# Queries and keys made transposed and split ahead of each attention, expert weights loaded during attention

## The chip, the cores and the metric

One core of a Trainium2 chip runs the whole program, a two-layer transformer block in one launch. Its engines are TensorE (PE), VectorE (DVE), ScalarE (ACT), GpSimd (POOL) and SyncE (SP, which here only issues DMAs). The metric is the device time of the core in microseconds: lower is better. The time before is the median of three runs; beside it there is one profiled execution, from which all rows come.

## The reference

The input x has 4 batches of 1024 tokens, 256 wide, so 4096 tokens. Each attention has 16 heads of 16.

```
x = x + LN(attention0(LN(x)))            # softmax(q k^T / 16) v, then w_out; no mask
x = x + LN(moe0(LN(x)))                  # twice: z += sum over 2 groups of expert(rmsnorm(z)); 8 experts, 512 wide, silu
x = x + LN(attention1(LN(x)))            # q,k,v with biases; scores + slope*(key - query), causal; w_out, bias
x = x + LN(balanced_experts(LN(x)))      # every expert gets 512 tokens; 1024 wide, gelu
```

Everything is float32. The scores are made to float32 accuracy from `fp32r` operands: a number is split in a high part (its `fp32r` rounding) and a low part (the rest), and q k is high x high + high x low + low x high, which one product of 64 rows per head can hold: the rows of q are [extra, high, high, low], those of k [extra, low, high, high] or the like, 16 rows each, and 5 extra rows (`AUG`) carry the running max and, in the second attention, the position term.

## The kernel before

The program is a chain of stages with a barrier of all engines between them: `ln_qkv` (tag qkv0), `attention` (att0), `attn_post`, then twice `rms_logits`, `route`, `experts`, then `combine_qkv` (qkv1), `attention` (att1), `attn_post`, and the assigned experts. The order on each engine is that in which the code is written; semaphores join the engines. `Mem` holds a stage's buffers and semaphores.

**qkv stages.** 32 tiles of 128 tokens. For each: norm (VectorE), two transposes (`turn`), products with 768 columns of w (`product`: the tile's xT is stationary, w moves), copy of the PSUM tile (`y_out`), a store of 384 KB to `qkv`. In qkv1 a product with two rows of ones adds the bias (L1239), in a part of 512 and one of 256 columns.

**Attention.** It works on couples of two heads, 8 for each batch and 32 in all. One couple takes a slot on TensorE, of NS steps: 16 in the first attention, 12 in the second, causal one. In a slot three couples are worked on: couple e has its products `qk` (L233) and `pv` (L249), the next couple m and the one behind it have their `scores` (L221) for the row maximum. `qk(n)` fills a PSUM bank that ScalarE's exp (L317) reads, `scores` fills one that VectorE's maximum (L357, causal: L363) reads; both draw on a ring of three banks S, and TensorE waits in L228 and L215 for the reader of the bank that it takes next. At step NS-4 `turn_max` (L263) transposes the couple's max, VectorE copies it to mT (L386), and SP's `place` (L115) puts it as a row into qT, for which the first `qk` of the next slot waits (m_placed). `finish` (L257) transposes the output for the division by the sum of exps (L371 to L377).

qT and kT are made inside the attention: SP loads rows of q and k (`load_qk`, L108) for two couples at once, GpSimd's `natural` splits them into qn and kn (token by token), TensorE's `fill` transposes half of one (four transposes, L206) into the bank TP, and ScalarE's `evac` (L314) copies it out. There are four fills in a slot: at n=0, at QUERIES0 = 2*CHUNK0 (8 and 4), at KEYS0-1 (10 and 6), and at NS-2. TP is shared with `finish`; `t_bank_read` (L199) waits for its last reader:

```
def fill(s,f,half):
    if f==1 and half==0: pe.wait_ge(nat_ready[s],1)...
    t_bank_read()
    for t in range(4): mm=pe.transpose(TP[...],(kn,qn)[f][:,s,4*half+t]...,identr[:])
    mm.then_inc(half_full,1)
```

**rms, route, experts.** `rms_logits` normalises 32 tiles and makes the routing logits. In the first of the two, ScalarE issues the loads of w1 and w2 (8 of 1 MB) ahead of its work, and every second tile carries one of 16 parts of 1024 columns: a high copy (ScalarE, L830) and the subtraction of it (VectorE, L859). Each of these stages loads its own constants, and VectorE and TensorE wait for them first. `route` makes one-hots for 64 columns of tokens in chunks of 8 (VectorE L1022, ScalarE L925), sums them on TensorE (L934), and writes `source`, `target` and the expert of each tile. `experts` gathers 128 rows for each of 72 tiles (GpSimd, L1063).

## Time and profile before

| what | us |
|---|---|
| median of three runs | 3442.67 (3439.02 to 3446.1) |
| profiled execution, its own time | 3440.81 |
| its span in the trace | 3438.9 |
| qkv0 from | 0 |
| att0 from | 109.24 |
| first post stage, first rms, route, experts from | 1002.65, 1116.9, 1200.1, 1267.65 |
| second rms, route, experts from | 1559.9, 1634.15, 1701.57 |
| qkv1 from | 1993.04 |
| att1 from | 2157.87 |
| second post stage from | 2850.5 |
| TensorE, VectorE, ScalarE, GpSimd busy | 2745.7, 1968.0, 1642.4, 931.7 |

A stage runs from the first event behind one barrier to that behind the next, and all engines wait for the slowest at each. TensorE is busy for 80% of the span, but that is a mean over stages with different limits; a stage must be read for itself. Times in rows are us from the span's start.

### The profile page before, as it was taken

What the parts mean: (1) busy time and instruction counts of PE and PEld (TensorE: products, weight loads), DVE (VectorE), ACT (ScalarE), POOL (GpSimd) and SP (SyncE); (2) the same over time, 40 slices, a digit from 0 to 9 for tenths busy, and PEclk for the clock granted to TensorE, in tenths of its full rate; (3) what the DMA queues carried; (4) which work ended last, traced back from release to release, by engine and by line L of the source; (5) the groups of instructions that cost most, each with busy time, mean ns of one, the idle gap of its engine ahead of it and who ended that gap; (6) DMA issues with size and microseconds to landing.
All of it is one profiled execution on the core that took longest, in us unless ns stands there. A gap on an engine that the chain in (4) does not pass through costs nothing. (4 is left out here: it accounts for less than half of the span.)

```text
span 3438.9 us, 63399 instructions
## 1 busy us (share of the span) xinstructions
PE 2745.7 (80%) x16332; PEld 1631.3 (47%) x16333; DVE 1968.0 (57%) x4576; ACT 1642.4 (48%) x2593; POOL 931.7 (27%) x1637
## 2 busy tenths in 40 slices
PE   8699999999975449995399959688888887718887
PEld 5333333333333438884388824344444444515554
DVE  4478887888845353335433354477666764555641
ACT  3277777777754434433344335366666663301212
POOL 1211111111016105541055444222222213302333
PEclk9699999999996559995599979799999996659999
DMA  6201010010023402225022257211111104322331
GB/s 167 58 20 25 12 25 19 19 25 19 12 58 100 156 10 70 68 61 150 16 67 69 64 148 195 52 26 25 25 31 28 28 10 118 114 96 69 98 99 60
DMA packets 367444, 216.00 MB, mean 63 GB/s; under 512 B 285262, under 2 KB 347218, under 8 KB 366295
## 3 DMA queue, kind: packets, MB, share of 16 engines
q1 hardware_dynamic: 231832, 99.25, 11.2%
q10 hardware_dynamic: 117568, 62.92, 6.1%
q0 software_dynamic: 17920, 52.46, 4.8%
q8 instruction: 43, 0.70, 0.1%
q14 instruction: 81, 0.66, 0.1%
HBM read 130.13 MB, written 85.98 MB: 63 GB/s over the span
## 5 line engine op out<-in xcount | busy, mean ns | idle before, releaser
L317 ACT ACTIVATE att_pr<-att_S 128x1024 f32<-128x1024 f32 (+1 forms) x896 | 835.9, 941 | 428.2 <-ACTq L324 426.4
L357 DVE TENSOR_REDUCE att_mparts<-att_S 128x2 f32<-128x1024 f32 x640 | 776.8, 1224 | 170.3 <-DVEq L353 166.3
L233 PE MATMUL att_S<-att_qT,att_kT 64*128 64x512 f32 (+3 forms) x1792 | 430.6, 473 | 45.4 <-PEq L228 41.8
L249 PE MATMUL att_OP<-att_pr,att_vn 128*32 128x512 f32 (+3 forms) x3584 | 451.9, 565 | 1.0 <-PEq L243 0.7
L221 PE MATMUL att_S<-att_kT,att_qT 64*128 64x512 f32 (+3 forms) x1792 | 390.9, 431 | 73.6 <-PEq L215 61.9
L233 PEld LDWEIGHTS att_S<-att_qT,att_kT 64*128 64x128 f32 x1792 | 175.0, 184 | 471.3 <-issue 460.3
L169 POOL COPY att_vn<-att_raw 128x256 f32<-128x256 f32 x64 | 25.4, 396 | 1150.0 <-POOLq L168 1150.0
L221 PEld LDWEIGHTS att_S<-att_kT,att_qT 64*128 64x128 f32 x1792 | 188.0, 191 | 172.7 <-issue 166.3
L363 DVE CUSTOM_DVE_ANT_0 att_unused<-att_S,att_mask 128x128 f32<-128x128 f32 (+3 forms) x512 | 228.4, 488 | 71.9 <-DVEq L353 71.8
L1063 POOL DMA_INDIRECT experts_xs<-scaled,ffn_source x144 | 140.3, 974 | 368.5 <-SPq L1056 172.2
L1163 DVE COPY experts_y<-experts_Y 128x256 f32<-128x256 f32 x144 | 61.1, 424 | 225.1 <-DVEq L1162 225.1
L1137 ACT ACTIVATE experts_hh<-experts_TH 128x512 fp32r<-128x512 f32 x144 | 86.1, 598 | 205.2 <-ACTq L1136 205.2
L1069 POOL DMA_INDIRECT mixed<-experts_y,ffn_target x144 | 146.2, 1015 | 88.6 <-issue 46.7
L1160 DVE TENSOR_TENSOR experts_hl<-experts_TH,experts_hh 128x512 fp32r<-128x512 f32 x144 | 99.6, 692 | 117.8 <-DVEq L1158 117.1
L1140 ACT ACTIVATE experts_h<-experts_H 128x512 f32<-128x512 f32 x144 | 86.1, 598 | 125.3 <-ACTq L1139 125.3
L1405 PE MATMUL ffn_Y<-ffn_w,ffn_hT 128*128 128x256 f32 x512 | 127.3, 399 | 8.8 <-PEq L1404 8.8
L1400 PE MATMUL ffn_H<-ffn_xT,ffn_w 128*128 128x512 f32 x256 | 120.4, 626 | 14.7 <-PEq L1398 8.7
L653 PE MATMUL post_Y<-post_w,post_aT 128*128 128x256 f32 x256 | 104.0, 549 | 33.4 <-PEq L651 33.4
L457 POOL TENSOR_TENSOR post_s<-post_s,post_half 128x2 f32<-128x2 f32 x128 | 96.2, 752 | 118.4 <-POOLq L629 112.5
L249 PEld LDWEIGHTS att_OP<-att_pr,att_vn 128*32 128x32 f32 x3584 | 72.2, 108 | 109.6 <-issue 105.2
L314 ACT ACTIVATE att_qT<-att_TP 128x512 fp32r<-128x512 f32 x128 | 76.1, 594 | 90.7 <-ACTq L312 90.7
L371 DVE TENSOR_REDUCE att_osum<-att_TP 128x136 f32<-128x272 f32 x128 | 56.2, 439 | 99.9 <-DVEq L369 99.9
(290 smaller groups left out, 4977.3 us busy)
## 6 DMA issues: line engine op xcount, KB each, us to landing
qkv<-qkv_y ACTq DMA_DIRECT2D x64, 384.0 KB, 3.9
att_raw<-qkv SPq DMA_DIRECT2D x96, 256.0 KB, 3.2
ffn_w<-in_w ACTq DMA_DIRECT2D x20, 1024.0 KB, 13.4
rows<-post_rows ACTq DMA_DIRECT2D x32, 384.0 KB, 2.8
ao<-att_aon SPq DMA_DIRECT2D x32, 256.0 KB, 2.3
post_at<-ao SPq DMA_DIRECT2D x64, 128.0 KB, 3.0
scaled<-rms_zs SPq DMA_DIRECT2D x64, 128.0 KB, 1.7
rms_rows<-mixed SPq DMA_DIRECT2D x32, 256.0 KB, 3.1
```

The lines of the kernel that those rows point to most:

```text
L221: mm=pe.matmul(S[:,b,h,at:at+n],qT[r,s,qt*128:qt*128+128],kT[r,s,half*512:half*512+n],start=True,stop=True)
L233: mm=pe.matmul(S[:,b,h,f:512],kT[r,s,kt*128:kt*128+128],qT[r,s,c*512+f:c*512+512],start=True,stop=not diag)
L249: mm=pe.matmul(OP[32*j:32*j+32,f:512],vn[:,s,kt,h,:],pr[:,n%4,h,f:512],start=kt<2,stop=g in last_groups,skip_group_check=True)
L317: nc.scalar.activation(pr[:,n%4,:,f:512],S[:,ring["e",n],:,f:512],ACT.Exp,scale=exp_scale).then_inc(s_free[ring["e",n]],1)
L357: nc.vector.tensor_reduce(mparts[:,s,:,2*qt+half],S[:,b,:,0:width(qt,half)],AX.X,ALU.max).then_inc(end,1)
L363: nc.vector.tensor_tensor_reduce(unused[:,2*i+h,0:n],S[:,b,h,at:at+n],mask[:,512-n:512],1.0,-3.0e38,ALU.add,ALU.max,mparts[:,s,h,2*qt+half ...
L653: mm=pe.matmul(Y[:,u%4,0:DIM],aT[:,u%2,128*k:128*k+128],w[:,k,:],start=k==0,stop=k==KC-1 and not last)
L1063: nc.gpsimd.indirect_dma_start(out=xs[:,t%R,:],out_offset=None,in_=zs_d,in_offset=bass.IndirectOffsetOnAxis(ap=source[:,t:t+1],axis=0)).th ...
L1069: nc.gpsimd.indirect_dma_start(out=y2_d,out_offset=bass.IndirectOffsetOnAxis(ap=target[:,t:t+1],axis=0),in_=y[:,t%RY,:],in_offset=None, bo ...
L1160: V.tensor_tensor(hl[:,u%2],TH[:,u%2,:],hh[:,u%2].bitcast(F32),ALU.subtract).then_inc(hT_ready,1)
L1400: mm=pe.matmul(H[:,c%2,:],w1[:,e%2,k,128*c:128*c+128],xT[:,k,:],start=k==0,stop=k==KC-1)
L1405: if c<FC: pe.matmul(Y[:,t%2,0:DIM],hT[:,c,128*t:128*t+128],w2[:,e%2,c,:],start=c==0,stop=False)
```

## The change

- `ln_qkv` and `combine_qkv` make q and k transposed: `features` takes 128 columns of w as the stationary operand and xT of four tiles (512 tokens) as the moving one, four steps behind `turn`. ScalarE copies the product to its high part, VectorE subtracts for the low part, and both go to DRAM `qk` (two 2 KB pieces of a row, 512 KB in each of 32 stores). v is made and stored by itself (`values`). In qkv1 the bias of q and k is added in these two instructions, and only v's 256 columns keep the product with ones.
- `attention` has no `natural`, `fill`, `evac`. It has four operand sets of qT and kT. SP's `load_set` fills one from `qk` by rows: 12 loads of 16 rows of 4 KB, and 2 rows of zeros (att0) or 4 loads of position rows (att1). It is issued three couples ahead, when TensorE gives a set free at n=2, and stands ahead of `place` in SP's program. `scores` of a couple wait for `set_loaded`. At the start GpSimd clears qT, VectorE clears kT and writes its two rows of -1, and only then are sets free.
- In att0 SP issues, behind the first three sets and the first values and ahead of the first `place`, the loads of w1, w2 and seven constants that the ffn stages now hold. GpSimd splits w1 in eight parts, four behind the first values and four at the end.
- `rms_logits` of the first loop splits only w2, eight parts, at every third step; no stage of the ffn loads constants. In `route` two of eight one-hots are made on VectorE directly, and the tile counts come last. In `experts` four gathers are issued at once, and the first product comes ahead of the second transpose.

```diff
 attention
-        qn=sb("qn",[128,2,TILES,2,WIDE],F32R); kn=sb("kn",[128,2,TILES,2,WIDE],F32R); identr=sb("identr",[128,128],F32R)
-        qT=sb("qT",[128,2,SEQ],F32R)
+        SETS=4
+        qT=sb("qT",[128,SETS,SEQ],F32R); kT=sb("kT",[128,SETS,SEQ],F32R)
...
+                def load_set(b,pair):
+                    s=pair%SETS; done=set_loaded[s]
+                    sp.wait_ge(set_free,1).then_inc(set_free,-1)
+                    for m,T,high,both in ((0,qT,AUG,AUG+HD),(1,kT,AUG+2*HD,AUG)):
+                        for h in range(2):
+                            to=lambda row,n: T[64*h+row:64*h+row+n,s,:].bitcast(F32)
+                            parts=qk_d[m][:,bass.ds(b*HEADS+2*pair+h,1)].bitcast(F32)
+                            sp.dma_start(to(high,HD),parts[0,0]).then_inc(done,16)
+                            for x in range(2): sp.dma_start(to(both+HD*x,HD),parts[x,0]).then_inc(done,16)
+                            if causal: sp.dma_start(to(0,AUG),augr[AUG*(2*pair+h):AUG*(2*pair+h)+AUG,m,:].bitcast(F32)).then_inc(done,16)
+                            elif m==0: sp.dma_start(to(0,1),zeros[:].bitcast(F32)).then_inc(done,16)
...
+                    if not (last and c+3>=COUPLES): load_set(*later(c+3))
...
+                    if not (last and c+1>=COUPLES): place(c+1)
+                for c in range(3): load_set(0,c)
+                load_v(0,0)
+                if ahead:
+                    for k in range(KC): sp.dma_start(w1[:,k,:].bitcast(F32),w1_d[128*k:128*k+128,:]).then_inc(w_loaded[k],16)
+                    sp.dma_start(w2[:].bitcast(F32),w2_d.rearrange("(k p) n -> p k n",p=128)).then_inc(held_loaded,16)
+                    for tile,value in zip(held,held_d): sp.dma_start(tile[:],value).then_inc(held_loaded,16)
+                place(0)
...
+                    if x==0: pe.wait_ge(set_loaded[s],16*LOADS).then_inc(set_loaded[s],-16*LOADS)
...
-                        if m is not None and n==0: fill(m,0,1)
-                        if a is not None and n==QUERIES0: fill(a,1,0)
-                        if a is not None and n==KEYS0-1: fill(a,0,0)
-                        if a is not None and n==NS-2: fill(a,1,1)
+                        if prev is not None and n==2: pe.sem_inc(set_free,1)
...
+                nc.vector.memset(kT[:].bitcast(F32),0.0).then_inc(dve_done,1)
...
+                for h in range(2): nc.vector.memset(kT[64*h:64*h+1].bitcast(F32),-1.0).then_inc(keys_cleared,1)
...
 ln_qkv
+                def low(b,u):
+                    dve.wait_ge(high_ready,1).then_inc(high_ready,-1)
+                    done(nc.vector.tensor_tensor(hl[:,u%HB,1],Q[:,u%2],hl[:,u%HB,0].bitcast(F32),ALU.subtract))
...
+                def features(b,u):
+                    f=u%4
+                    pe.wait_ge(q_free,1).then_inc(q_free,-1)
+                    for k in range(KC):
+                        mm=pe.matmul(Q[:,u%2],w[:,k,128*f:128*f+128],xT[:,k,u//4,:],start=k==0,stop=k==KC-1)
+                pipelined(pe,[turn,values,None,None,features])
...
 rms_logits
-            for i in range(16):
-                q=i//4; at=slice(1024*(2*q+i%2),1024*(2*q+i%2)+1024); raw,high=flat[0:2] if i%4<2 else flat[2:4]
-                parts[SCALED+4+2*i]=(q if i%4==0 else None,raw[:,at],high[:,at])
+            for i in range(8): parts[SCALED+2+3*i]=slice(1024*i,1024*i+1024)
```

The first place is TensorE's program in the second attention, at steps 4 to 6 of a slot: `att_S<-att_qT,att_kT` is `qk`, `att_S<-att_kT,att_qT` is `scores`, `att_TP<-att_identr` a fill, `att_TP<-att_ident` is `finish`. Before:

```order
L233 MATMUL att_S<-att_qT,att_kT 128x512 x2
L221 MATMUL att_S<-att_kT,att_qT 128x128 x2
L221 MATMUL att_S<-att_kT,att_qT 128x256 x2
L206 MATMUL att_TP<-att_identr,att_qn 128x128 x4
L257 MATMUL att_TP<-att_ident,att_ot 128x128 x4
L233 MATMUL att_S<-att_qT,att_kT 128x512 x2
L221 MATMUL att_S<-att_kT,att_qT 128x384 x2
```

And now:

```order
L221 MATMUL att_S<-att_qT,att_kT 128x512 x2
L209 MATMUL att_S<-att_kT,att_qT 128x128 x2
L209 MATMUL att_S<-att_kT,att_qT 128x256 x2
L245 MATMUL att_TP<-att_ident,att_ot 128x128 x4
L221 MATMUL att_S<-att_qT,att_kT 128x512 x2
L209 MATMUL att_S<-att_kT,att_qT 128x384 x2
```

The fill is gone, and `finish` follows the `scores` directly; the rest stands as it stood.

The second place is SP's program in the first attention, from the identity (before) or from the end of the third set (now) to the first `place`, which is `att_qT<-att_mT`. Before:

```order
L101 DMA att_ident<-in_ident 128x128
L108 DMA att_raw<-qkv 128x8x64 x2
L111 DMA att_raw<-qkv 128x8x64
L108 DMA att_raw<-qkv 128x8x64 x2
L115 DMA att_qT<-att_mT 1x8x128 x2
```

And now:

```order
L118 DMA att_kT<-qk 16x1024 x2
L123 DMA att_raw<-v 128x8x64
L146 DMA ffn_w<-in_w_0 128x4096 x2
L147 DMA ffn_w<-in_w_0 128x4x2048
L148 DMA ffn_ident<-in_ident 128x128
L148 DMA ffn_wg<-in_w_route 128x2x12
L148 DMA ffn_nw<-in_norm_w 128x256
L148 DMA ffn_trif<-in_prefix 128x256
L148 DMA ffn_key<-in_order 128x128
L148 DMA ffn_jv<-in_starts 128x576
L148 DMA ffn_marks<-in_marks 128x192
L127 DMA att_qT<-att_mT 1x8x128 x2
```

Three loads of weights and seven of constants now stand ahead of the first `place`, on the same queue.

The third place is ScalarE's program in the first rms stage. Before:

```order
L821 ACTIVATE rms_sq,rms_ss<-l_z 128x256
L826 ACTIVATE rms_zT<-rms_T 128x256
L830 ACTIVATE ffn_w1h<-ffn_w 128x1024
L821 ACTIVATE rms_sq,rms_ss<-l_z 128x256
L826 ACTIVATE rms_zT<-rms_T 128x256
L821 ACTIVATE rms_sq,rms_ss<-l_z 128x256
L826 ACTIVATE rms_zT<-rms_T 128x256
L830 ACTIVATE ffn_w1h<-ffn_w 128x1024
```

And now:

```order
L779 ACTIVATE ffn_w2h<-ffn_w 128x1024
L772 ACTIVATE rms_sq,rms_ss<-l_z 128x256
L777 ACTIVATE rms_zT<-rms_T 128x256
L772 ACTIVATE rms_sq,rms_ss<-l_z 128x256
L777 ACTIVATE rms_zT<-rms_T 128x256
L772 ACTIVATE rms_sq,rms_ss<-l_z 128x256
L777 ACTIVATE rms_zT<-rms_T 128x256
L779 ACTIVATE ffn_w2h<-ffn_w 128x1024
```

A part stood at every second tile, sixteen in all; it stands at every third now, eight in all, and the eight weight loads ahead of the first square are gone.

## Rows read from the trace of the kernel before

**Rows 1.** Windows: engine busy time (x instructions), PEclk, DMA share, GB/s.
```profile
150.00:160.00 10.00, 8.78 (x36) 4.06 (x34) 8.38 (x7) 5.07 (x6) 2.64 (x7) 0.50 0.12 27
150.00:1000.00 850.00, 766.42 (x4835) 304.50 (x4833) 661.47 (x749) 604.22 (x698) 116.10 (x262) 0.99 0.08 18
2200.00:2850.00 650.00, 567.00 (x4817) 305.16 (x4813) 439.23 (x1353) 400.31 (x568) 127.23 (x320) 0.99 0.11 24
```
**Rows 2.** Line L263 in each attention: ns min/median/max, first and last start.
```profile
L263 PE MATMUL att_S<-att_ident,att_m x32: 269/269/370, 148.0 to 970.3; 128*16 128x128 f32 x32
L263 PE MATMUL att_S<-att_ident,att_m x32: 269/270/372, 2191.8 to 2821.5; 128*16 128x128 f32 x32
```
**Rows 3.** Timeline of TensorE, first attention: start, us, engine, line, operation [idle].
```profile
565.67 0.53 PE L206 MATMUL att_TP<-att_identr,att_qn 128*128 128x128 f32 x4
...
566.81 0.51 PE L221 MATMUL att_S<-att_kT,att_qT 64*128 64x512 f32 x2 [0.18 <-PEq L215]
```
**Rows 4.** Timeline of ScalarE, the same stretch.
```profile
565.64 1.02 ACT L317 ACTIVATE att_pr<-att_S 128x1024 f32<-128x1024 f32 x1 [1.28 <-ACTq L324]
```
**Rows 5.** Timeline of TensorE, second attention, n=4 and 5.
```profile
2430.31 0.63 PE L257 MATMUL att_TP<-att_ident,att_ot 128*128 128x128 f32 x4 [1.10 <-PEq L199]
...
2431.20 0.34 PE L221 MATMUL att_S<-att_kT,att_qT 64*128 64x384 f32 x2
```
**Rows 6.** Timeline of ScalarE, the same stretch.
```profile
2429.57 0.59 ACT L314 ACTIVATE att_qT<-att_TP 128x512 fp32r<-128x512 f32 x1
```
**Rows 7.** Timeline of SP, second attention.
```profile
2417.08 1.37 SPq L115 DMA_DIRECT2D att_qT<-att_mT  x2
2419.05 1.01 SPq L108 DMA_DIRECT2D att_raw<-qkv  x2
```
**Rows 8.** Timeline of VectorE, start of the first route stage.
```profile
1204.42 0.27 DVE L945 MEMSET route_zero<- 128x256 f32 x1 [5.33 <-DMA route_marks<-in_marks]
```
**Rows 9.** DMA queues of 1115:1145: packets, MB, share.
```profile
q10 hardware_dynamic: 1152, 8.39, 68.7%
```
**Rows 10.** Timeline of all engines, first placing of a max.
```profile
149.34 1.49 SPq L115 DMA_DIRECT2D att_qT<-att_mT  x2
...
152.51 0.80 PE L233 MATMUL att_S<-att_qT,att_kT 64*128 64x512 f32 x2 [0.82 <-PEq L228]
```
**Rows 11.** Timeline of ScalarE, first rms stage.
```profile
1121.43 0.42 ACT L821 ACTIVATE rms_sq<-l_z 128x256 f32<-128x256 f32 x1 [3.25 <-issue]
...
1135.31 0.38 ACT L826 ACTIVATE rms_zT<-rms_T 128x256 f32<-128x256 f32 x1 [0.62 <-ACTq L825]
...
1136.48 0.38 ACT L826 ACTIVATE rms_zT<-rms_T 128x256 f32<-128x256 f32 x1 [0.39 <-ACTq L825]
...
1140.66 0.38 ACT L826 ACTIVATE rms_zT<-rms_T 128x256 f32<-128x256 f32 x1 [1.39 <-ACTq L825]
...
1144.85 0.38 ACT L826 ACTIVATE rms_zT<-rms_T 128x256 f32<-128x256 f32 x1 [1.39 <-ACTq L825]
```
**Rows 12.** Timeline of ScalarE and VectorE, end of the first route.
```profile
1258.63 5.52 ACT L925 ACTIVATE route_named<-route_in_slot,route_zeros,route_marks 128x72 fp32r<-128x72 f32 x16 [0.15 <-ACTq L922]
...
1262.21 1.20 DVE L943 TENSOR_REDUCE route_ef<-route_ge 128x72 f32<-128x576 f32 x1
```
**Rows 13.** Timeline of GpSimd, start of the first expert stage.
```profile
1272.68 0.95 POOL L1063 DMA_INDIRECT experts_xs<-scaled,ffn_source  x1 [2.75 <-POOLq L1062]
```
**Rows 14.** Timeline of SP, start of the second rms stage.
```profile
1564.84 6.45 SPq L799 DMA_DIRECT2D rms_rows<-mixed  x6
```
**Rows 15.** Timeline of TensorE, first qkv stage.
```profile
61.70 2.75 PE L562 MATMUL qkv_Y<-qkv_w,qkv_xT 128*128 128x512 f32 x8
```
**Rows 16.** Timeline of TensorE, second qkv stage.
```profile
2060.92 0.50 PE L1239 MATMUL qkv_Y<-qkv_biasr,qkv_ones 2*128 2x512 f32 x1
...
2062.72 0.44 PE L1230 MATMUL qkv_T<-qkv_ident,qkv_xn 128*128 128x128 f32 x2
...
2066.60 0.44 PE L1230 MATMUL qkv_T<-qkv_ident,qkv_xn 128*128 128x128 f32 x2
```

More of the change, by code:

```diff
@@ L190, in _ @@
+                if ahead:
+                    for i in range(PARTS//2): split(i)
+                with pool.Fori(1,BATCH*GROUPS):
+                    group()
+                if ahead:
+                    for i in range(PARTS//2,PARTS): split(i)
+                    pool.wait_ge(low_done,PARTS)
+                    pool.wait_ge(held_loaded,16*(1+len(held)))
             @block.tensor
             def _(pe):
-                pe.sem_inc(nat_free[0],1); pe.sem_inc(nat_free[1],1); pe.sem_inc(v_free[0],1); pe.sem_inc(v_free[1],1)
+                pe.sem_inc(v_free[0],1); pe.sem_inc(v_free[1],1)
@@ L1217, in root_x @@
                     root(nc,pool,half,sx[:,n%R],pool_done,rootx)
-                for n in range(NT+3):
-                    for lag,stage in ((0,root_z),(3,root_x)):
+                for n in range(NT+2):
+                    for lag,stage in ((0,root_z),(2,root_x)):
                         if 0<=n-lag<NT: stage(n-lag)
@@ L1278, in _ @@
-                done(V.tensor_scalar(low[:],low[:],ident[0:2,1:2],None,ALU.mult))
-                done(V.scalar_tensor_tensor(out=biasr[:],in0=high[:].bitcast(F32),scalar=ident[0:2,0:1],in1=low[:],op0=ALU.mult,op1=ALU.add))
+                done(V_.memset(ones[:].bitcast(F32),1.0))
+                done(V_.tensor_copy(split[:],bias[:]))
+                done(V_.tensor_tensor(rest[:],bias[:],split[:].bitcast(F32),ALU.subtract))
+                done(V_.tensor_scalar(rest[:],rest[:],ident[0:2,1:2],None,ALU.mult))
```

601 lines of the change are left out of this document (267 added, 334 removed).

## Prediction

> **What bounds the kernel now.** I read the busy time by windows first, then the order of events inside one slot of each attention, then the starts of the stages. In the long middle of both attentions TensorE is busy nine tenths of the time, more than any other engine [rows 1]: 766 of 850 us in the first, 567 of 650 us in the second. So work off TensorE's path is worth nothing there, and work on it is worth its length, less what comes back as another wait. The transposes of the max (one in each slot) give the slot: (970.3 - 148.0)/31 = 26.5 us in the first attention, (2821.5 - 2191.8)/31 = 20.3 us in the second [rows 2]. Attention holds 1586 of the 3439 us. The other stages are short, and their starts are waits.
>
> **Steady slots, first attention.** Out go four groups of four transposes (L206), some 0.46 us of TensorE each, and four ScalarE copies. 4 x 0.46 x 31 would be 57 us if it all lay on the path. The order of events says otherwise. Each fill stands behind `scores` of an even step; ahead of the next `scores` TensorE waits for the bank that exp reads. Exp starts at 565.64 and takes 1.02; the `scores` that need its bank start at 566.81, 0.15 behind its end, and TensorE still waited 0.18 with the fill in the gap [rows 3, 4]. Without the fill the same `scores` start at the same time: the fill is covered by the exp. What is gained is where the ScalarE copy delays an exp. I take 0.2 us a slot, -6 in all, with 0 and 0.5 (-16) as its ends.
>
> **Steady slots, second attention.** Half of the exps are shorter than 1024 columns, and the cover is thinner. Behind a fill, `finish` (L257) at 2430.31 had waited 1.10 us for ScalarE to have copied the shared bank TP: the copy starts at 2429.57, behind an exp that ends at about 2429.67, and takes 0.59 [rows 5, 6]. `scores` of the next step start at 2431.20. Without fill and copy, `finish` starts 0.46 us earlier plus those 1.10, and `scores` then wait only for that exp's end plus 0.15, so till 2429.8: 1.4 us gained. The fill at n=6 has no `scores` of an odd step behind it and is bare, 0.46; that at n=10 is bare for 0.1, that at n=0 is hidden by VectorE's row max. That is 2.0 us a slot of TensorE's path. Part comes back: VectorE's masked row maxima are queued close behind, and TensorE meets them sooner. Bounds: 0.65 if only the 0.2 to 0.5 us rests survive, 1.8 if nearly nothing is given back. I take 1.1, for 31 slots -34 (-20 to -55).
>
> **Can the row loads keep up?** A slot now needs 14 loads (16 in the second attention, plus store and values in every second slot, 17 on average) on SP's queue ahead of `place`, where 3 stood in two slots. Two loads issue in 1.01 us, two of `place` in 1.37 [rows 7], so 0.5 us each, at worst 0.69. SP may begin at n=2, some 4 us into the slot, and the placed max needs about 1.4 + 1.7 us behind it: 4 + 17c + 3.1 us. At c=0.5 that is 15.6, at 0.69 18.8 us, both under 19.2. The 64 KB loads of 16 pieces of 4 KB are smaller than the 256 KB of 256-byte pieces that those rows show, so I take 0.5 and no cost. The Trainium skill (DMA: Bandwidth & Descriptors, Rules for kernel authors) says that under 64 KB one pays mostly overhead; at its fixed 2 us for each, one after another, the 16 loads would take 32 us and bound the slot, an estimate from that page. That is a rival below, priced from rows.
>
> **Starts of the attentions.** VectorE's memset of 256 columns takes 0.27 us [rows 8], some 0.83 ns a column above the fixed part; kT has 4096 columns, and three such memsets (all, then one row for each head) are 10.3 us. Only then may SP load. 14 issues of 0.5 and 2 us of landing: first `scores` at +19.4 us, against +17.5 before: +2. In the second attention the copy of the position rows (2048 columns, 1.7 us by the same rate) stands ahead too, and 16 issues: +4.
>
> **Weights ahead of the first `place`.** This is the term that speaks against the change. SP issues three sets (42 x 0.5 = 21 us), the values, then 8.39 MB of w1 and w2 and 0.80 MB of constants, and only then `place(0)`, on one queue. Before, eight weight loads moved 8.39 MB with 68.7% of the DMA time of 30 us, so 0.41 MB/us [rows 9]. The weights begin at +10.4+21.5+1.5 = +33.4 and end 22.6 us later, at +56. Before, `place` was issued at 149.34 (+40.1) and the first `qk` ran at 152.51 (+43.3) [rows 10]; now it could run at +45.2. If `place` is served behind the weights, `qk` starts at +56.5: 11 us more. If it is served beside them, 0. The trace of before has no small transfer behind megabytes on its own queue to read it from. By the Trainium skill (DMA: Bandwidth & Descriptors, Queues, rings and completion order) each DMA engine consumes the descriptors of one ring in order, which gives the 11; its rule that different rows are served in turn would have given 0 had the weights stood on another queue. I take 11. TensorE's granted clock was still 0.50 in 150:160 with the first couple under way [rows 1]; 11 us of idleness there keep it low longer. I add 3 us for it. Sum of the start: 2 + 11 + 3 = +16.
>
> **First rms stage.** ScalarE issued eight loads until 1121.43 before its first square; block start 1116.9, less 1.3 for the table load that stays: -3.1. A tile without a split takes 1.17 (1135.31 to 1136.48), two tiles with one split 4.19 (1140.66 to 1144.85) [rows 11]: a split costs 4.19 - 2.34 = 1.85. Eight of sixteen remain: -14.8. Together -18. The w1 splits run on GpSimd in the attention, idle there for most of the time: nothing.
>
> **Route, experts, second rms.** Route's VectorE waits for constants until 1204.42, 4.2 us behind its start at 1200.1 [rows 8]; these are held now: -4.2. ScalarE makes 16 one-hots in 5.52 [rows 12], 0.345 each; two of eight move to VectorE, whose pace then bounds: I take 0.3 of the possible 0.69 for 8 chunks, -2.4, and -1.2 for the first chunk's order. The tile counts, hidden until now, come behind the targets: a reduce of 1.20 [rows 12], a compare of the same tile and two short ones, I take +2.9. Per route -4.9, two: -9.8. Experts: the second gather waited 2.75 us [rows 13]; issued back to back, and the first product ahead of the second transpose: -2.5, twice -5. Second rms: rows are fetched at 1564.84 behind the constants though the stage begins at 1559.9 [rows 14]: -4.4.
>
> **The two qkv stages.** TensorE's columns stay the same: 2.80 us a tile in the first [rows 15]. But `features` lag four steps, so four steps run at VectorE's pace (I estimate 2.0) and four blocks of 1.75 are left at the end: 8.1 + 28 x 2.8 + 7 = 93.5 against 89.6: +4. In the second a tile takes 3.88 (2062.72 to 2066.60), with 0.43 for the bias product of 512 columns [rows 16], which goes; VectorE's own work grows by the 128x512 subtraction, 0.7, to about 3.55, just above TensorE's 3.45. 4 x 2.9 + 28 x 3.55 + 7 = 118 against 124.5, with 1.5 for the shorter bias preparation: -8. Ends: -14 and +2, the latter if the longer chain of waits (features, high, low, free) costs 0.3 a tile.
>
> **Sum.** 4 + 16 - 6 - 18 - 9.8 - 5 - 4.4 - 8 + 4 - 34 = -61. Against the profiled execution's 3440.8 that is 3380; the median of the runs lies 2 us above it, within their spread, so 3380 stands for it too.
>
> **Rivals.**
> (a) The fills were worth more: both attentions gain near their upper bounds (-16, -55) and `place` is served beside the weights (0, no clock loss). 3380 - 10 - 21 - 14 = 3335. For: VectorE was busy only 68% of the second attention. Against: waits for VectorE already stand between the steps. 0.17.
> (b) VectorE takes the fills' place in the second attention (about 0 there) or the qkv stages lose: 3380 + 34 = 3414, or 3390. The ffn stages alone still gain 37. 0.20.
> (c) Slower: issue of the row loads bounds the second attention. At c=1.0 us the slot is 4 + 17 + 3.1 = 24.1, +3.8 for 31 slots: 3380 + 34 + 118 = 3530. It decides from c = 0.83, where the slot is 21.2 us and all other gains are eaten. For: nothing that size was issued before. Against: no row above 0.69 in the steady part. 0.09. Another 0.02 for an issue cost near that point, where gain and loss cancel.
> (d) As summed, between 3350 and 3400: 0.52.
>
> **How the numbers follow.** 3380 is (d). The range takes in (a) and most of (b): 3332 to 3412. Some 0.2% (7 us) is what a measurement of this kernel can tell from no change. (a), (b) and (d) all lie below 3436: faster 0.89; the 0.02 is the same; (c) is slower, 0.09.
>
> **What would show it.** First `qk` of the first attention at +56 (right) or +45 (the queue serves `place` beside the weights). SP's issues near 0.5 us each. Slot of the second attention 19.2 us, of the first 26.3; behind `finish` no wait for ScalarE, more waits for VectorE. First rms 18 us shorter. Wrong if SP is still issuing when the max is ready, if waits for `set_loaded` show at TensorE, or if a qkv tile takes over 4 us.

## The result and the profile after

| | before | after |
|---|---|---|
| median of the runs on one chip | 3440.85 (3430.84 to 3446.1) | 3731.13 (3725.98 to 3736.39) |
| ratio | 1 | 1.0848 (1.0823 to 1.0874) |
| profiled execution, its span | 3440.81, 3438.9 | 3728.71, 3726.6 |

The kernel became 8.5% slower; the forecast was 3380, so 1.8% faster, with 3332 to 3412 as its range. Each kernel of the experiments was timed beside the kernel before on one chip. Its number is given against the median of the kernel before in that sitting (3431.7 to 3437), with the ratio and its 95% interval.

First the page of the changed kernel, its totals and TensorE's row of the 40 slices (one digit is 93 us), and behind them the same row of the kernel before (86 us):

```profile
PE 2744.7 (74%) x15276; PEld 1572.5 (42%) x15277; DVE 2021.0 (54%) x4669; ACT 1509.1 (40%) x2361; POOL 708.6 (19%) x1074
...
PE   5554888888887646996499946648888887736887
...
PE   8699999999975449995399959688888887718887
```

The rows hint where to look: the first three slices of the changed kernel hold TensorE at 5 tenths, where the first slice of the kernel before has 8, and those of its second qkv stage (slices 24 to 27) have 4 to 6. Other slices are as low in both kernels, so the stage lengths decide. They are taken, from one table load of ScalarE to the next (us; the terms of the forecast's sum beside them):

| stage | before | after | difference | forecast |
|---|---|---|---|---|
| qkv0 | 108.5 | 282.7 | +174.2 | +4 |
| att0 | 893.4 | 912.8 | +19.4 | +10 (start +16, steady -6) |
| rms0 | 83.2 | 64.1 | -19.1 | -18 |
| route0, route1 | 67.6, 67.4 | 65.8, 66.2 | -3.0 | -9.8 |
| experts0, experts1 | 292.2, 291.5 | 288.2, 287.3 | -8.2 | -5 |
| rms1 | 74.3 | 71.2 | -3.1 | -4.4 |
| qkv1 | 164.8 | 295.6 | +130.8 | -8 |
| att1 | 692.7 | 690.1 | -2.6 | -30 (start +4, steady -34) |
| post0, post1, ffn1 | | | -0.7 | 0 |

The differences add up to 287.7, and by so much the span is longer. The two qkv stages alone lose 305; the rest of the kernel gained 17. Each stage is read from one trace, and identical code does not take the same time in every trace: in the eight traces here whose second attention is that of the changed kernel, this stage takes 688.5 to 698.1. So its -2.6 is no difference from before.

**The first qkv stage.** The waits of the changed kernel from 0 to 330 us (engine, line, whose event ended the wait: us in total, times, longest):

```profile
DVE qkv_hl L490 <- DVEq L489: 184.4, 32, 7.3
PE qkv_T L504 <- PEq L502: 118.9, 30, 9.3
```

L490 is `low`, VectorE's subtraction; L489 is its wait for ScalarE's `high`. L504 is `turn`, which waits for the normalised tile. Each waits in each tile. One tile in the timeline (start, us, engine, line, operation, idle before):

```profile
104.67 0.60 ACT L533 ACTIVATE qkv_hl<-qkv_Q 128x512 fp32r<-128x512 f32 x1 [2.99 <-ACTq L532]
...
105.41 0.69 DVE L490 TENSOR_TENSOR qkv_hl<-qkv_Q,qkv_hl 128x512 fp32r<-128x512 f32 x1 [7.11 <-DVEq L489]
106.55 0.43 DVE L485 BATCH_NORM_STATS2 qkv_st<-qkv_xt 128x6 f32<-128x256 f32 x1 [0.44 <-DVEq L483]
...
107.71 0.41 DVE L494 TENSOR_SCALAR qkv_xn<-qkv_xt,qkv_st 128x256 f32<-128x256 f32 x1
...
108.42 0.66 PE L504 MATMUL qkv_T<-qkv_ident,qkv_xn 128*128 128x128 f32 x2 [3.96 <-PEq L502]
...
108.97 2.05 PE L511 MATMUL qkv_V<-qkv_w,qkv_xT 128*128 128x256 f32 x4
...
110.80 1.92 PE L517 MATMUL qkv_Q<-qkv_xT,qkv_w 128*128 128x512 f32 x2
...
114.63 0.60 ACT L533 ACTIVATE qkv_hl<-qkv_Q 128x512 fp32r<-128x512 f32 x1 [3.03 <-ACTq L532]
...
115.37 0.69 DVE L490 TENSOR_TENSOR qkv_hl<-qkv_Q,qkv_hl 128x512 fp32r<-128x512 f32 x1 [7.25 <-DVEq L489]
```

Read it as a ring: `low`, the statistics, `normal`, `turn`, `values`, `features`, `high`, `low`. From one `low` to the next 9.96 us pass, and little overlaps. From the sixth tile on, 8.0 to 10.4 us lie between one `turn` and the next, 9.2 on average. Before, a tile took 2.80. The granted clock is lower too. One window of the changed kernel's first stage (us, busy time of PE, PEld, DVE, ACT, POOL, then PEclk, DMA share, GB/s):

```profile
100.00:150.00 50.00, 29.73 (x55) 14.41 (x54) 9.34 (x25) 7.20 (x16) 2.74 (x5) 0.70 0.24 79
```

**The second qkv stage.** The waits of 2170 to 2440:

```profile
POOL qkv_sz L432 <- POOLq L1164: 152.8, 26, 8.6
DVE qkv_hl L1258 <- DVEq L1257: 150.1, 30, 7.8
ACT qkv_lnz L1206 <- ACTq L1205: 149.6, 31, 6.1
```

Three engines each wait some 150 us of 270. The profile names only the waiting line; what it waits for is read from the program: GpSimd's roots for VectorE's statistics, ScalarE's `ln_z` for the roots, VectorE's `low` (L1258) for ScalarE's `high`. `turn` starts at 2378.73 and again 9.10 us later, where it had come every 3.88 [rows 16]:

```profile
2378.73 0.66 PE L1181 MATMUL qkv_T<-qkv_ident,qkv_xn 128*128 128x128 f32 x2 [3.73 <-PEq L1178]
...
2387.83 0.66 PE L1181 MATMUL qkv_T<-qkv_ident,qkv_xn 128*128 128x128 f32 x2 [2.84 <-PEq L1178]
```

**The start of the first attention.** The stage begins at 283.43. SP's timeline from the weights to the first `place` (L127), which answers to [rows 10]:

```profile
321.87 1.90 SPq L148 DMA_DIRECT2D ffn_nw<-in_norm_w  x1
323.81 4.79 SPq L148 DMA_DIRECT2D ffn_trif<-in_prefix  x1
328.64 2.72 SPq L148 DMA_DIRECT2D ffn_key<-in_order  x1
331.40 0.43 SPq L148 DMA_DIRECT2D ffn_jv<-in_starts  x1
331.88 6.91 SPq L148 DMA_DIRECT2D ffn_marks<-in_marks  x1
338.90 1.49 SPq L127 DMA_DIRECT2D att_qT<-att_mT  x2
```

TensorE, the same stretch:

```profile
327.37 0.37 PE L250 MATMUL att_S<-att_ident,att_m 128*16 128x128 f32 x1 [2.04 <-PEq L249]
...
346.13 0.79 PE L221 MATMUL att_S<-att_qT,att_kT 64*128 64x512 f32 x2 [16.07 <-PEq L216]
```

The max was transposed at 327.37. SP was still issuing constants, and four of these issues held it 1.9 to 6.9 us where another of the same line takes 0.4. Before, the same load of `in_marks`, with no weights ahead of it, held SP for 0.43. `place` was issued at +55.5, and the first `qk` ran at +62.7, 19.4 later than before. The first `scores` had come at +22.9 (before +17.5). Ahead of them VectorE's timeline has the three memsets, which had been taken for 10.3 us in all and take 3.47 each with gaps:

```profile
284.37 3.47 DVE L310 MEMSET att_kT<- 128x4096 f32 x1 [5.12 <-PEq L29]
...
288.94 3.47 DVE L313 MEMSET att_kT<- 1x4096 f32 x1 [1.02 <-DVEq L312]
293.31 3.47 DVE L313 MEMSET att_kT<- 1x4096 f32 x1 [0.91 <-issue]
```

**The steady second attention.** Two windows, and two single microseconds of the second:

```profile
2700.00:2740.00 40.00, 33.29 (x284) 16.75 (x278) 29.26 (x90) 21.75 (x29) 0.88 (x3) 1.00 0.23 59
2900.00:2940.00 40.00, 34.23 (x270) 16.86 (x268) 27.72 (x84) 20.82 (x28) 0.80 (x2) 0.91 0.22 54
...
2902.00:2903.00 1.00, 0.01 (x1) 0.00 (x0) 0.84 (x4) 0.94 (x2) 0.00 (x0) 1.00 0.46 127
2903.00:2904.00 1.00, 0.86 (x6) 0.46 (x10) 0.81 (x2) 0.00 (x0) 0.00 (x0) 0.61 0.11 33
2904.00:2905.00 1.00, 1.00 (x8) 0.02 (x3) 0.71 (x4) 0.98 (x1) 0.00 (x0) 0.50 0.46 131
```

TensorE there, at step 7 of a slot:

```profile
2903.14 0.75 PE L221 MATMUL att_S<-att_qT,att_kT 64*128 64x512 f32 x2 [1.13 <-PEq L216]
2903.82 1.94 PE L237 MATMUL att_OP<-att_pr,att_vn 128*32 128x512 f32 x8
```

The same step ten slots earlier, and what VectorE and ScalarE did ahead of 2903.14:

```profile
2705.41 0.49 PE L221 MATMUL att_S<-att_qT,att_kT 64*128 64x512 f32 x2 [1.13 <-PEq L216]
2705.83 1.06 PE L237 MATMUL att_OP<-att_pr,att_vn 128*32 128x512 f32 x8
...
2901.93 1.02 ACT L291 ACTIVATE att_pr<-att_S 128x1024 f32<-128x1024 f32 x1
...
2902.28 0.55 DVE L332 CUSTOM_DVE_ANT_0 att_unused<-att_S,att_mask 128x384 f32<-128x384 f32 x1
```

The wait of 1.13 us stands in both. Three banks of S are handed out in turn, so this `qk` takes the bank of the `scores` of 384 columns at step 5. Its reader is VectorE's masked maximum, which ends at 2902.83. The exp that runs beside it reads another bank, that of step 6. So the wait is for VectorE. At 2705 the granted clock stays at 2.4 GHz and the eight `pv` take 1.06; at 2903 it falls to 1.2 GHz for some 3.6 us and they take 1.94. Slots of the first kind last 19.18 and 19.92 in turn, of the second 20.41 and 20.55; before, all took about 20.3 at a granted clock of 0.97 to 1.00. The wait stands in 30 slots. The clock held behind 13 of them and fell behind 17, the last 13 of the stage among these.

### The profile page after: what moved, and what is told of

The parts are those of the page before. It is cut to its first block and busy times, and to the rows that moved or that the text cites. A ratio compares the mean times of both kernels' runs of the same rounds, so it can differ in the third digit from the quotient of the medians.

```text
span 3726.6 us, 61821 instructions
## 1 busy us (share of the span) xinstructions
PE 2744.7 (74%) x15276; PEld 1572.5 (42%) x15277; DVE 2021.0 (54%) x4669; ACT 1509.1 (40%) x2361; POOL 708.6 (19%) x1074
## 5 line engine op out<-in xcount | busy, mean ns | idle before, releaser
L291 ACT ACTIVATE att_pr<-att_S 128x1024 f32<-128x1024 f32 (+1 forms) x896 | 826.2, 940 | 642.7 <-ACTq L297 640.8
L221 PE MATMUL att_S<-att_qT,att_kT 64*128 64x512 f32 (+3 forms) x1792 | 438.5, 479 | 138.2 <-PEq L216 132.3
L237 PE MATMUL att_OP<-att_pr,att_vn 128*32 128x512 f32 (+3 forms) x3584 | 466.8, 583 | 1.1 <-PEq L231 0.7
L490 DVE TENSOR_TENSOR qkv_hl<-qkv_Q,qkv_hl 128x512 fp32r<-128x512 f32 x32 | 22.1, 692 | 184.4 <-DVEq L489 184.4
L1380 PEld LDWEIGHTS ffn_Y<-ffn_w,ffn_hT 128*128 128x128 f32 x512 | 95.2, 194 | 32.2 <-issue 20.4
```

Source lines behind the costliest of these rows:

```text
L221: mm=pe.matmul(S[:,b,h,f:512],kT[r,s,kt*128:kt*128+128],qT[r,s,c*512+f:c*512+512],start=True,stop=not diag)
L237: mm=pe.matmul(OP[32*j:32*j+32,f:512],vn[:,s%2,kt,h,:],pr[:,n%4,h,f:512],start=kt<2,stop=g in last_groups,skip_group_check=True)
L291: nc.scalar.activation(pr[:,n%4,:,f:512],S[:,ring["e",n],:,f:512],ACT.Exp,scale=exp_scale).then_inc(s_free[ring["e",n]],1)
L1380: if c<FC: pe.matmul(Y[:,t%2,0:DIM],hT[:,c,128*t:128*t+128],w2[:,e%2,c,:],start=c==0,stop=False)
```

## The experiments

**The ring in the first qkv stage.** My theory was that `low` of tile n-5, which VectorE does in the same step as `normal` of n-1, waits for a product that TensorE does only behind `turn` of the tile that `normal` has just given. The rivals were that the work itself, the row stores of 2 KB pieces, or the lower granted clock bound the tile. One step more of lag keeps all work and all traffic:

```diff
-                pipelined(dve,[x_stats,normal,None,None,None,low])
+                pipelined(dve,[x_stats,normal,None,None,None,None,low])
```

> Only the first qkv stage is edited: VectorE takes `low` of a tile six steps behind, not five. Theory (a loop in program order): in one step VectorE runs the norm of tile n and then waits for the high copy of tile n-4, whose product stands behind the transposes of tile n on TensorE, so nothing overlaps and a tile costs the whole chain, 9 to 10 us. With one step more the loop is open: a tile then costs 2.9 to 3.3 us, the stage goes from 283 us to 105 to 120, the kernel from 3731 to 3555 to 3575. Rival A (the 512 KB stores and their landing set the pace) expects no change, since the stores are the same. Rival B (TensorE's lower granted clock, 0.7 to 0.83 here, lengthens the stage by itself) expects no change either, or some 20 us. Rival C (SP's order, where each load waits behind the store eight tiles older) expects a tile still above 6 us.

> The same edit with seven steps. If only the loop mattered, six and seven steps give the same within 5 us. If the wait for the high copy still shows at six, seven is up to 10 us shorter: VectorE then paces a tile at about 2.9 us. If SP's loads, which stand behind the store of the tile eight steps older, come too late for it, seven is slower than six and VectorE waits for x at its statistics.

Measured with six: 3585.96 against 3436.99, 1.043 (1.041 to 1.0451); with seven 3579.25, 1.0411 (1.039 to 1.0432). The stage falls from 282.7 to 131.9 and 127.5. One `None` is worth 151 us with every instruction and every store kept, so the ring is shown, and the granted clock is back at 1.00 (10 to 110 us; 0.77 in the changed kernel), so it had followed the ring. The size was a miss: 105 to 120 us had been expected of six, and 3555 to 3575 of the kernel. What remains is some 3.6 us a tile, TensorE with the kernel of six:

```profile
61.58 0.41 PE L504 MATMUL qkv_T<-qkv_ident,qkv_xn 128*128 128x128 f32 x2 [0.44 <-PEq L502]
...
65.10 0.41 PE L504 MATMUL qkv_T<-qkv_ident,qkv_xn 128*128 128x128 f32 x2 [0.25 <-PEq L502]
```

**The same cure in the second.** There ScalarE's step begins with `ln_z`, which waits for statistics that VectorE makes at the end of a step, and ends with `high`, for which VectorE waits at the start of the next.

```diff
                 def step(at):
+                    if at(7): high(*at(7))
                     if at(0): ln_z(*at(0))
...
-                    if at(7): high(*at(7))
```

> Only the second qkv stage is edited: in ScalarE's step the high copy comes first, ahead of ln_z, ln_x, the copy of the transposes and v. Theory: `low`, which stands first in VectorE's step, waits for a high copy that stands behind ln_z of the step before, which waits through GpSimd's root for the statistics at the end of that very VectorE step; the loop VectorE, GpSimd, ScalarE, VectorE makes 9.1 us a tile. With the high copy first a tile costs 3.6 to 4.5 us, the stage 295.6 goes to 130 to 160, the kernel to 3565 to 3600. Rivals A (stores) and B (clock) expect under 30 us of change.

Measured: 3709.99, 1.0791 (1.0764 to 1.0818). The stage fell by 19 to 276.2, where 130 to 160 had been expected. The waits of 2170 to 2420 show why:

```profile
ACT qkv_hl L1218 <- ACTq L1217: 162.0, 28, 7.0
...
DVE qkv_hl L1258 <- DVEq L1257: 123.7, 28, 7.1
```

ScalarE's wait went from `ln_z` to `high` itself: it now stands first, ahead of `turned`, and waits for `features`, which has only two Q banks and stands behind the `turn` of that step. The edit moved the ring and did not open it. My expectation had looked at one engine's order and not at the whole ring.

> Both edits (six steps in the first stage, high copy first in the second). Theory: the two gains add up, 3731 - 170 - 145 = 3415, with 3395 to 3440; the rest of the change is then seen to be worth 0 to 45 us against the kernel before. A rival in which one stage's slowness only hides a wait of the other is excluded by the barriers between stages, so a sum that is missed by over 10 us would need another cause.

Both edits together: 3559.38, 1.0349 (1.0332 to 1.0366), outside the 3395 to 3440 expected, since the second cure had failed. The stages take 132.0 and 276.1, what they took alone, so the gains add.

Then the lags and the banks of both: Q has four PSUM banks, in the second stage `high` is done at 8, `low` and the store at 10; in the first `low` is done at 7, as in the run with seven, and the stores of q and k are issued by ScalarE. Of the edit, the part on the second stage:

```diff
-        T=m.ps("T",[128,2,512]); Q=m.ps("Q",[128,2,512]); V=m.ps("V",[128,2,512])
+        T=m.ps("T",[128,2,512]); Q=m.ps("Q",[128,4,512]); V=m.ps("V",[128,2,512])
...
-                    if at(7): high(*at(7))
...
+                    if at(8): high(*at(8))
...
-                    if at(8): keep_block(*at(8))
-                stepwise(act,8,step)
+                    if at(10): keep_block(*at(10))
+                stepwise(act,10,step)
...
-                LOW=8
+                LOW=10
```

> Both qkv stages, with the loops opened wider: four PSUM buffers for the feature products instead of two; first stage: `low` seven steps behind, stores of the blocks issued by ScalarE; second stage: high copy eight steps behind in its old place (behind ln_z and ln_x), `low` and the store ten behind. The run with the high copy first showed that it only swapped loops: 133 us of VectorE waits for the high copy stayed, since ScalarE then waited for TensorE's whole tile before it made the next norm. Theory: only slack of more than one step on every side opens it. Then the second stage takes 3.9 to 4.2 us a tile, 165 to 180 us instead of 295.6; the first 2.9 to 3.1 a tile, 108 to 118 us. Kernel 3731 - 170 - 120 = 3441, within 3425 to 3455. Rival: 512 KB stores or the GpSimd roots set a floor, then the second stage stays above 200 us.

Measured: 3472.53 against 3435.8, 1.0114 (1.008 to 1.0148), outside the 3425 to 3455 expected. The second stage fell to 180.3, the upper end of what was expected: 115 us came from buffers and lags alone, with the same work and stores, so a ring of waits is shown there too. Which of the lags and banks opened it was not separated. The first came to 146.1, worse than with six (131.9) or seven (127.5): that half was a miss, and is taken up below.

**The start of the first attention.** Theory: SP, held up by issues behind the weights, is what delays the first `place`. Rival: the memsets and the row loads. `place(0)` was put ahead of the weight loads; in the other kernel ScalarE issues the weights and constants at the start of the stage.

```diff
+                place(0)
                 if ahead:
...
-                place(0)
```

> First attention only: the first `place` stands ahead of the ten loads of weights and constants on SP, else nothing. The first qk ran 62.7 us into the stage (before: 43.3). If the loads ahead cause it (SP is held up while it issues the constants until 55.5 us, and the placed max lands 7 us behind its issue), it now runs at 45 to 50 us, and the stage loses 12 to 17 us, unless the next couple's `place`, which then stands behind the weights, takes it over: then the gap appears one slot later and the stage loses under 5 us. Kernel 3714 to 3728.

```diff
-                    for k in range(KC): sp.dma_start(w1[:,k,:].bitcast(F32),...)
...
+                    for k in range(KC): act.dma_start(w1[:,k,:].bitcast(F32),...)
...
```

> First attention only: the same ten loads are issued by ScalarE at the stage's start, on its queue, instead of by SP. If a small transfer on SP's queue is served beside megabytes on another, the first qk runs at 45 to 50 us and the stage loses 13 to 18 us. If the DMA engines are shared so that the 14 loads of the first set get slow beside the weights, the first `scores` come later than 24 us and the gain is smaller. ScalarE has no exp to do until the first qk, so its issues cost nothing.

place_first: SP issues `place` at 331.96, the first `qk` runs at 335.13, +48.6 where the stage starts at 286.5, and the stage is 11.5 shorter, just under the 12 to 17 expected. That shows the order on SP as the cause of 14 of the 19 us by which the first `qk` was late; the rest, +5.3, stands in the memsets and row loads ahead. The whole kernel measured 3721.27, 1.0839 (1.0795 to 1.0882), which can't be told from the changed kernel's 1.0848: in this trace the second attention, whose code is the same, took 698.1 for 690.1. w_act: the stage is 6.5 shorter, not 13 to 18 (3731.2, 1.0867, 1.0832 to 1.0903). SP is free, but the first `scores` came at 318.45, +30.8 for +22.9, and the first `qk` at +56.3: the first row loads, issued at the same place in the stage, went beside 8.39 MB of weights and took longer. So both costs are real, and the order on SP, not another queue, is the better cure.

**The clock in the second attention.** Two kernels add the same eight transposes to each slot, whose result nobody reads (they leave nothing out); the first at step 6, ahead of the wait at step 7, the second at step 3.

```diff
+                        if causal and e is not None and n==6:
+                            pe.wait_ge(t_free,1)
+                            for t in range(8): pe.transpose(TP[:,128*(t%4):128*(t%4)+128],ident[:],ident[:])
```

> Second attention only: eight transposes of the identity without a reader (about 0.9 us) are added on TensorE at step 6, where it waits 1.13 us for VectorE at the next qk. Theory: without fills the slot is 19.2 and 19.9 us long by turns as long as the granted clock stays 1.00 (mean 19.55), and 20.5 where the clock falls to 0.50 for some 3.5 us of the slot, each time right behind that wait; the extra work keeps the clock at 1.00 and all slots at about 19.55 to 19.7: 20 of 31 slots gain 0.85, the stage 690 goes to 670 to 676 although TensorE does more. Rival (VectorE's chain alone sets 20.4 in these slots, the clock only follows): no change or up to +28 us (31 x 0.9) for the added work.

> Second attention only: the same eight transposes as in the run that keeps TensorE at work, but at step 3, where TensorE waits 0.3 us at most for VectorE. If the clock falls because of the one long wait before the qk of step 7, these transposes don't help: the falls stay, and TensorE has up to 0.9 us more to do in each slot: the stage takes 690 to 715 us. If any added work keeps the clock, or if added work changes the phase of the engines, the stage is as short as with the transposes at step 6 (674) plus what isn't covered, 675 to 690.

warm: 3708.38 against 3435.8, 1.0801 (1.0761 to 1.0841); the stage fell from 690.1 to 673.9 though TensorE does more. One window:

```profile
2900.00:2940.00 40.00, 34.95 (x302) 18.63 (x303) 28.38 (x89) 21.78 (x29) 0.80 (x2) 1.00 0.25 63
```

All slots from 2690 on take between 18.95 and 20.33, 19.51 on average, with the granted clock at 1.00: the changed kernel's slots of the first kind, now throughout. The 16 us are the price of the low clock, and this price changes from trace to trace: in the eight traces with this stage's code unchanged the clock fell in some 15 to 25 slots, and the stage took 688.5 us where it fell least often and 698.1 where it fell most often.

warm_at3: 3739.27 against 3431.7, 1.0896 (1.0877 to 1.0916), stage 705.6. The number lies where I had put it for a clock that keeps falling, but in the trace the clock mostly holds. One window:

```profile
2900.00:3000.00 100.00, 84.99 (x709) 44.97 (x708) 69.10 (x214) 52.95 (x69) 2.00 (x5) 0.98 0.21 53
```

TensorE at step 3 and at step 7 of one of its slots:

```profile
2911.25 1.09 PE L265 MATMUL att_TP<-att_ident 128*128 128x128 f32 x8
2912.27 1.07 PE L237 MATMUL att_OP<-att_pr,att_vn 128*32 128x512 f32 x8
...
2917.95 0.49 PE L221 MATMUL att_S<-att_qT,att_kT 64*128 64x512 f32 x2 [1.13 <-PEq L216]
2918.37 1.06 PE L237 MATMUL att_OP<-att_pr,att_vn 128*32 128x512 f32 x8
```

The wait of 1.13 stands in 30 slots, as in the changed kernel, and the clock falls behind 5 of them, not 17. What costs is that the transposes stand bare, 1.02 us (2911.25 to 2912.27): slots at full clock take 20.3 on average where those of warm take 19.4, so 0.9 more in each, and the five falls add to it, which together is the 31 us. So work at step 3 keeps the clock up too, a little less surely than work inside the wait (5 falls against none), and there it is not free. What lets the clock fall in one slot and not in another with the same wait is not settled by these runs.

**Fewer memsets at the start.** The second attention overwrites both rows of -1 with its position rows, and the first can have one written by GpSimd beside VectorE's other:

```diff
+                if not causal:
...
+                    nc.gpsimd.memset(kT[64:65].bitcast(F32),-1.0).then_inc(keys_cleared,1)
...
-                for h in range(2): nc.vector.memset(kT[64*h:64*h+1].bitcast(F32),-1.0).then_inc(keys_cleared,1)
+                if causal: dve.sem_inc(keys_cleared,2)
+                else:
+                    dve.sem_inc(all_clear,1)
+                    nc.vector.memset(kT[0:1].bitcast(F32),-1.0).then_inc(keys_cleared,1)
```

> Only the clearing of kT at the attentions' starts is edited: in the second attention the two rows of -1 aren't written (the position rows bring them), in the first GpSimd writes one of the two beside VectorE. The three memsets take 3.47 us each with 0.9 us between them. Theory: they stand ahead of every load, so the first set of the first attention is issued 4.4 us earlier and that of the second 8.7 us earlier: stages 912.8 to 909.5 or less (the weights ahead of the first place may take part of it back), 690 to 682. Rival (the loads wait for something else, as the barrier or the constants): no change.

Measured: 3708.13, 1.0806 (1.0786 to 1.0825); first attention 907.1 (-5.7), second 677.7 (-12.4). In the first the `scores` start 4.3 us earlier, as expected. In the second the first `qk` had come at +46.4 for +38.3 before; it now comes at +41.1, so 5.3 earlier, not 8.7. The other 7 us of the -12.4 stand in the slots, 19.8 us on average for 20.0: the clock fell behind 8 waits for 17. Nothing in the edit touches the slots, and whether it changed this number or the trace was a lucky one stays open. So the memsets are worth 5.3 of the second's +8.1 at the start.

**All of it.** The kernel best joins qkv_open, place_first, warm and starts, and ScalarE does the store at the head of its step, eight steps behind:

```diff
+                    if at(8): keep(*at(8))
                     if at(0): turned(*at(0))
...
-                    if at(7): keep(*at(7))
```

> All edits at once: qkv loops opened (as in the run with four buffers, but in the first stage the store comes first in ScalarE's step, eight tiles behind, since there it waited for VectorE's step of the same number and made a new loop: 146 us against 127.5), the first place ahead of the weights, the extra transposes at step 6 of the second attention, and the shorter clearing. Sum by stages against the kernel before (3436): qkv 118 and 178 for 108.5 and 164.8: +23; first attention 898 for 893: +5; second 667 for 693: -26; rms, route and expert stages -34. Together 3404, within 3390 to 3420, so 0.5 to 1.3% faster than before. If the clock falls again in the shorter slots, up to 20 us more.

Measured: 3445.57 against 3431.7, 1.0037 (1.0024 to 1.0051), outside the 3390 to 3420 expected: of the 290 us between the medians 276 are back, and it is still just slower than before. The first stage stayed at 145.5, where 118 had been expected. Its timeline shows the wait (ScalarE's issue of a store, and its next `high`):

```profile
63.23 0.40 ACTq L553 DMA_DIRECT2D qk<-qkv_hl  x1
...
66.17 0.60 ACT L546 ACTIVATE qkv_hl<-qkv_Q 128x512 fp32r<-128x512 f32 x1 [1.75 <-ACTq L545]
```

`high` of tile n-4 needs the buffer of tile n-8 (there are four, `HB`), whose store was issued in the same step: 2.94 us from issue to `high`, about the landing of a store (3.1 us by the page of the profile), stood in the ring of every tile. In the run with seven, where SP issued the stores, the stage had taken 127.5. So twice as many buffers:

```diff
-HB=4
+HB=8
```

> The kernel with all edits, and eight buffers instead of four for the split blocks (hl). In the run with all edits the first qkv stage still took 145.5 us, 4.3 a tile: its high copy starts 2.94 us behind the issue of the store of the tile eight steps back (63.23 to 66.17), whose buffer it takes, step after step, so the landing of that store is part of a loop. Theory: with eight buffers the landing is off the path; a tile then costs 2.8 to 3.1 us, the first stage 110 to 120, the second 165 to 178 for 179.4. Kernel 3445 - 30 - 5 = 3408, within 3392 to 3425, so faster than before by 0.2 to 1.2%. Rival (ScalarE's own work with two DMA issues a tile sets 4.3 us): no change, 3440 to 3448.

Measured: 3416.47 (3410.04 to 3421.76) against 3435.35, 0.994 (0.9925 to 0.9956). That is within the 3392 to 3425 expected. The stage falls from 145.5 to 120.7 (expected 110 to 120), its tile from some 4.0 to 3.2 us, so the landing in the ring is shown. The second stage, which has the eight buffers too, stays at 180.0. `turn` on TensorE in the first:

```profile
60.68 0.41 PE L517 MATMUL qkv_T<-qkv_ident,qkv_xn 128*128 128x128 f32 x2
...
63.84 0.41 PE L517 MATMUL qkv_T<-qkv_ident,qkv_xn 128*128 128x128 f32 x2
```

That is 0.6% faster than the kernel before and 8.4% faster than the changed one (0.994/1.0848). Against before its stages differ by: qkv +12.2 and +15.1, first attention +1.9, second -18.0, first rms -19.3, second -3.0, routes and experts -11.2, the rest +3.4; together -18.9. A trace is one execution: that of best was its fastest, 14 us under its median, and that of best_eight its slowest, so the two spans differ by 10 us only, and stages with the same code by up to 6.

## Why the prediction was wrong

The forecast missed the profiled run by 349 us: 170 in qkv0, 139 in qkv1, 27 in the second attention, 9 in the first, and 3 in the rest.

- **The two qkv stages: the step that failed.** "TensorE's columns stay the same ... four steps run at VectorE's pace" took each stage for a pipe whose pace is that of its busiest engine. It put the longer chain of waits at nothing in the first stage, and at "0.3 a tile" as the far end of the second. Measured: 6.4 us a tile in the first stage (9.2 for 2.8), 5.2 in the second (9.1 for 3.88). Neither the columns (the tile is 3.2 us once the ring is open) nor VectorE's work were at fault: each engine's program has its order, `low` of an old tile waits for a product that stands behind `turn` of the tile just normalised, and the next `normal` stands behind that `low`. This could have been found from the program alone: write down, for one step, what each engine does in order and for which tile, and follow it round until it comes back to its start; the lag it comes back with is the number of tiles in flight, here one. The sign that the prediction gave for itself, a qkv tile of over 4 us, named the right number, but no rival stood behind it: rival (b) let the qkv stages lose 10 us at most (3390), and the one slower rival, 0.09, was about another queue.
- **The -8 of the second qkv stage:** it can't be seen beside 131 us. In the best kernel the stage is still 15 us longer than before, so the -8 did not come; what holds it there was not looked into.
- **Weights ahead of the first `place`: right in kind, short in size.** The first `qk` was forecast 13 us later (11 for the queue, 2 for memsets and loads) and came 19.4 later. The order on SP was the cost of 14, as place_first shows. SP still issuing when the max is ready was one of the prediction's signs of being wrong, and here it was. What I missed is that SP itself is held up (6.91 us for one constant), and the gaps of 1 us between the memsets: +13.8 to SP's first load where I had 10.4. The 3 us for the clock were too much: with the first `qk` under way, 23.3 us pass to the next transposed max, where 22.4 had passed before.
- **Steady first attention: the mechanism right, the size at its end.** Forecast -6 with 0 as an end; the slots are 26.46 on average for 26.51, so -1 in all. The fills were under the exp, as [rows 3, 4] say.
- **Steady second attention: the gain was there, and the clock took it back.** Forecast 1.1 a slot; at full clock it is 20.3 - 19.5 = 0.8. In the changed kernel some 16 us of that go to the low clock (690.1 against 673.9), and the start took 8.1 where 4 was forecast. Together: -25 + 16 + 8 = -1, for -2.6 measured. Against [rows 5], where `finish` waited 1.10 for ScalarE, no wait stands ahead of `finish` now; in its place `qk` waits 1.13 for VectorE's masked maximum at step 7. That part comes back as a wait for VectorE was forecast, and is right. The forecast had the clock as a cost at the start alone, and did not ask what idle time in the middle would do to it.
- **Row loads (rival c): refuted.** 16 loads take SP from 2698.40 to 2707.27, so 0.55 each with gaps (I had 0.5, and 0.83 as the deciding point), and SP is ready before the max. Timeline of SP:

```profile
2698.40 0.33 SPq L117 DMA_DIRECT2D att_qT<-qk  x1
...
2706.56 0.71 SPq L119 DMA_DIRECT2D att_kT<-att_augr  x1
...
2709.37 1.39 SPq L127 DMA_DIRECT2D att_qT<-att_mT  x2
```

  They land in 2.1 to 2.3 us and overlap. The Trainium skill (DMA: Bandwidth & Descriptors, Rules for kernel authors) warns of loads under 64 KB; these are 64 KB each, and 20 KB for the position rows. Taken as a fixed cost of 2 us one after another it would have given 32 us, an estimate, and the trace shows 8.87 for the 16.
- **First rms stage: right**, -19.1 for -18. The first square starts 1.29 behind the start of the table load, as reckoned from [rows 11].
- **Second rms and experts: about right**, -3.1 for -4.4 and -8.2 for -5. Four gathers now go out 1.25 to 1.5 us apart, where the second had waited 2.75 [rows 13].
- **Routes: wrong by a factor of three**, -3.0 for -9.8. The wait for constants is gone: VectorE's first memset starts at 1374.35, 0.1 behind the stage's start, for the 4.3 of [rows 8]. The chunks are what failed: they come every 2.88 us where they had come every 2.84, and VectorE makes two one-hots more in each; that its work took the place of ScalarE's is the likely cause, not tested. The size of the tail was not read by itself.

## What to carry to other kernels

Before costing a software pipeline by its busiest engine, write one step of every engine with the tile of each operation, and follow each value back through the program order of the engines; a ring that closes with a lag of one tile makes the sum of all latencies the pace, and one more step of lag or more buffers, not less work, cured it here. Work that is taken off TensorE may have been what kept its clock up: look at the granted clock in single microseconds after the change, and if it falls, put work that costs nothing inside a wait. Look at one stage in several traces before you read a few us from it. Put the small transfer that a loop waits for ahead of the megabytes on its queue, and count the store's landing when you choose the number of buffers.

## What the runs showed of the hardware

- The granted clock fell from 2.4 to 1.2 GHz for some 3.6 us behind a wait of 1.13 us in 17 slots and held in 13 others behind the same wait; with eight more transposes a slot it fell in none when they filled the wait, and in 5 of 30 when they stood elsewhere.
- The same code of the second attention took 688.5 to 698.1 us in eight traces, the more the more often the clock fell (15 to 25 slots).
- The issue of a load of constants that held SP for 0.43 us held it for 6.91 us behind 8.39 MB of loads on its queue.
- A memset of 4096 columns takes VectorE 3.47 us on 1 partition as on 128.
- A `high` that reuses a buffer started 2.94 us behind the issue of its store; twice as many buffers were worth 25 us in a stage of 32 tiles.
